# Expert weights of a routed decoder layer: all requested at the start, measured and split in earlier steps

## The reference, cut to what matters

```
x = layernorm(x + attention(x))             # 16 heads of 8, softmax, bias bo on the output
x = layernorm(x + retention(x, ctx, ctx))   # rotated queries and keys, decay mask, 16 heads of 8
x = layernorm(x + ffn(x))
ffn: 8 experts; each token takes its top 2 by x @ gate, softmax of the two logits as weights
     expert e: (silu(x @ w1[e]) * (x @ w3[e])) @ w2[e],  w1, w3: 128 x 512,  w2: 512 x 128
```

## Time and profile before

| | |
|---|---|
| median of the runs | 1030.12 us |
| profiled execution | 1043.64 us, span 1041.8 us from first to last instruction |
| busy over the span | PE 841.7, DVE 800.1, ACT 619.4, POOL 650.2 us |
| moved by DMA | 72.09 MB, mean 69 GB/s |
| mean granted clock of TensorE | 0.921 |

### The profile page before, as it was taken

One profiled execution on the slowest core, in us unless ns is written; L12 is line 12 of the kernel. 1 busy time (PEld: TensorE's weight loads), 2 busy tenths in 40 slices (PEclk: granted clock), 3 DMA queues, 4 the chain that ended last, 5 costly groups with the idle time before them and its releaser, 6 DMA issues.

```text
span 1041.8 us, 35968 instructions
## 1 busy us (share of the span) xinstructions
PE 841.7 (81%) x12164; PEld 632.6 (61%) x12165; DVE 800.1 (77%) x2219; ACT 619.4 (59%) x1416; POOL 650.2 (62%) x738
## 2 busy tenths in 40 slices
PE   1574879999999999988979760899999999999600
PEld 1342556666666666665655430788888888888500
DVE  3876889998889888978956644587878888778565
ACT  1132547667677676666666851566666666666445
POOL 0363957689889998989896456144444444444443
PEclk9796989999999999999998975899999999999955
DMA  7232312132222321212212002222212212212177
GB/s 240 59 75 66 69 30 49 32 73 54 58 64 52 70 63 48 68 33 63 48 48 62 23 27 82 53 63 58 57 57 58 58 56 61 58 53 61 34 253 228
DMA packets 145256, 72.09 MB, mean 69 GB/s; under 512 B 75024, under 2 KB 134544, under 8 KB 145136
## 3 DMA queue, kind: packets, MB, share of 16 engines
q1 hardware_dynamic: 124800, 40.56, 16.7%
q0 software_dynamic: 8640, 17.84, 5.1%
q10 hardware_dynamic: 11696, 12.08, 3.7%
HBM read 42.11 MB, written 28.34 MB: 68 GB/s over the span
## 4 chain that ended last, share of the span: by engine, by line
PE 33%; POOL 25%; issue 15%; DMA 3%; ACT 1%; SPq 1%; DVE 1%; POOLq 0%; another core or an unknown queue 0%; ACTq 0%; DVEq 0%
POOL prod_ev L1550 14%; PE QKV L770 9%; PE ST L770 9%; POOL routed_rows L1567 7%; PE XT L798 6%; PE SC L798 5%; POOL rs L1530 2%; DMA prod_ev<-token_halves 1%; PE YY L788 1%; DMA routed_rows<-xe,pos 1%; PE TR L788 1%; POOL frs L1612 1%; PE ST L640 1%; PE YY L588 1%; SPq L488 0%
## 5 line engine op out<-in xcount | busy, mean ns | idle before, releaser
L1550 POOL TENSOR_TENSOR prod_ev<-e_sb,q_v 128x512 f32<-128x512 f32 x256 | 296.1, 1189 | 85.1 <-PE YY L588 47.9
L1599 POOL DMA_INDIRECT token_halves<-w_new,tok_i x142 | 137.9, 971 | 39.7 <-issue 34.1
L1567 POOL DMA_INDIRECT routed_rows<-xe,pos x128 | 130.7, 1021 | 30.4 <-issue 30.0
L1150 DVE TENSOR_TENSOR prod_qk<-q_v,QKV 128x2048 f32<-128x2048 f32 x64 | 145.5, 2275 | 0.0
L1036 ACT ACTIVATE prod_qk<-QKV,silu_scale 128x512 f32<-128x512 f32 x142 | 95.1, 687 | 60.4 <-PE QKV L770 58.9
L1452 DVE TENSOR_TENSOR prod_ev<-prod_qk,prod_ev 128x1024 f16<-128x1024 f32 x71 | 87.0, 1225 | 54.7 <-ACT prod_ev L1027 35.2
L770 PE MATMUL QKV<-k_t,w_hl 128*128 128x256 f16 x852 | 117.4, 274 | 0.1
L770 PE MATMUL ST<-k_t,w_hl 128*128 128x256 f16 x852 | 117.0, 274 | 0.1
L411 POOL TENSOR_TENSOR marks<-half_c 128x1 f32<-128x1 f32 x103 | 19.7, 192 | 151.2 <-DVE w_new L1468 150.9
L1478 DVE SCALAR_TENSOR_TENSOR prod_qk<-ST,hid_scale,prod_qk 128x512 f32<-128x512 f32 x142 | 102.1, 744 | 10.0 <-ACT prod_qk L1036 6.5
L923 ACT ACTIVATE q<-XT,tab 128x256 f32<-128x256 f32 x256 | 96.6, 496 | 0.0
(11 more groups left out here) (169 smaller groups left out, 1776.7 us busy)
## 6 DMA issues: line engine op xcount, KB each, us to landing
w_new<-routed_rows SPq DMA_DIRECT2D x71, 130.0 KB
prod_ev<-token_halves SPq DMA_DIRECT2D x16, 512.0 KB, 5.0
x_sb<-x SPq DMA_DIRECT2D x32, 128.0 KB, 2.6
x_res<-x SPq DMA_DIRECT2D x128, 32.0 KB
head_rows<-o_n SPq DMA_DIRECT2D x32, 128.0 KB
o_t<-head_rows SPq DMA_DIRECT2D x64, 64.0 KB
ctx_sb<-ctx SPq DMA_DIRECT2D x32, 128.0 KB
out<-prod_qk ACTq DMA_DIRECT2D x16, 256.0 KB, 4.2
```

The source lines that it names most:

```text
L1150: eng.tensor_tensor(prod_qk[:, u, :, :].rearrange("p d (i j) -> p d i j", j=NH), q.unsqueeze(3).to_broadcast([P, HD, NH, NH]), k.unsqueeze ...
L1550: ins = eng.tensor_tensor(prod_ev[:, u, q, :, :, 0:HD], e_sb[:, it.slot(2), u, 64 * q:64 * q + 64].rearrange("p (i j) -> p j i", j=4).unsq ...
L1567: eng.indirect_dma_start(out=xs, out_offset=bass.IndirectOffsetOnAxis(ap=pos[:, r, 2 * u + k:2 * u + k + 1], axis=0), in_=xe[:, r, u, k, : ...
L1599: eng.indirect_dma_start(out=halves, out_offset=bass.IndirectOffsetOnAxis(ap=tok_i[:, s, u:u + 1], axis=0), in_=yw[:, s, u, :], in_offset= ...
```

## The change

All three matrices are requested by ScalarE before its first wait, in the order w1, w2, w3: six requests, 6 MB. w1 keeps `w_new`; w3 keeps `q8`; w2 goes to the memory of `w3_hl`, which is as large (two halves of 4096 float16 a partition) and is not needed for itself until the high half of w3 is written. The blank write stays at the end of ScalarE's step 0. The matrices are handled in the order w1, w2, w3, and the steps become (0, 3, 5), (3, 5, 7), (3, 5, 7), (4, 6, 8). The high half of w3 waits for the low half of w2 (`lo_ready` 2), and the first write of q8 in retention waits for `lo_ready` 3 where it waited for 2. SyncE no longer waits for `pool_consts` 2 ahead of the x tiles. TensorE starts on `consts_ready` 1 (the constants that VectorE copies at lines 1064 and 1065) and waits for `consts_ready` 2 (the bias rows) in `residual` of item 0. No instruction of arithmetic is added or removed.

```diff
--- before.py
+++ after.py
@@ -412,6 +412,8 @@
 
         def fresh(n):
 
+            if n == 2:
+                return w3_hl[:, :, :].rearrange("p k w -> p (k w)").bitcast(F32)
             return q8[:, :, :, :, :, :].rearrange("p s b u r t -> p (s b u r t)") if n == 1 else w_new[:, :]
 
         def norm_slot(c, d):
@@ -432,7 +434,8 @@
 
 
 
-        MEASURE, SPREAD_AT, HIGH, LOW, FETCH_LAST = (1, 3, 6), (3, 5, 8), (3, 5, 8), (4, 6, 9), 5
+        MEASURE, SPREAD_AT, HIGH, LOW = (0, 3, 5), (3, 5, 7), (3, 5, 7), (4, 6, 8)
+        WEIGHTS = (0, 2, 1)
         SPREAD = ST[:, 0:P]
 
         def pairs(ap):
@@ -450,8 +453,6 @@
             eng.dma_start(wo_sb[:, :], wo).then_inc(small_in, 16)
             eng.dma_start(bo_sb[:, :], bo).then_inc(small_in, 16)
             eng.dma_start(gate_sb[:, :], gate).then_inc(small_in, 16)
-
-            eng.wait_ge(pool_consts, 2)
 
             def step(at):
                 if it := at(0):
@@ -526,7 +527,7 @@
         def _(eng):
             eng.wait_ge(tab_in, 16)
             eng.wait_ge(small_in, 16 * 4)
-            eng.wait_ge(consts_ready, 2)
+            eng.wait_ge(consts_ready, 1)
 
             def tokens_across(it):
 
@@ -591,6 +592,8 @@
 
             def residual(it):
 
+                if it.i is None and it.off == 0:
+                    eng.wait_ge(consts_ready, 2)
                 wait_ring(it, y_in, per=96)
                 wait_last(it, n_duo, (x2t_ready, 5), (res1_ready, 1))
                 eng.matmul(Y, ones_bf[:, :], bo_bf[:, :], start=True, stop=False, skip_group_check=True)
@@ -701,12 +704,12 @@
 
             def spread_max(at):
 
-                for n in range(3):
-                    if at_step(at, SPREAD_AT[n]):
-
-                        eng.wait_ge(mats_ready, n + 1)
-                        if n > 0:
-                            eng.wait_ge(top_ready, n)
+                for k in range(3):
+                    if at_step(at, SPREAD_AT[k]):
+
+                        eng.wait_ge(mats_ready, k + 1)
+                        if k > 0:
+                            eng.wait_ge(top_ready, k)
                         eng.matmul(SPREAD, w_mats[:, :], ident, start=True, stop=True).then_inc(max_spread, 1)
 
             def step(at):
@@ -813,7 +816,6 @@
         @block.scalar
         def _(eng):
             w2_parts = w2.rearrange("e (n p) h -> n p e h", p=P)
-
             def load_weights(n):
 
                 if n < 2:
@@ -821,8 +823,11 @@
                                   (w1, w3)[n].rearrange("e h i -> h e i")).then_inc(w_in[n], 16)
                 else:
                     for k in range(n_chunk):
-                        eng.dma_start(w_new[:, :].rearrange("p (e n h) -> p e n h", e=n_exp, n=n_chunk)[:, :, k, :],
+                        eng.dma_start(fresh(n).rearrange("p (e n h) -> p e n h", e=n_exp, n=n_chunk)[:, :, k, :],
                                       w2_parts[k]).then_inc(w_in[n], 16)
+
+            for n in WEIGHTS:
+                load_weights(n)
 
             eng.wait_ge(tab_in, 16)
             eng.wait_ge(small_in, 16 * 4)
@@ -830,20 +835,16 @@
             def weights(at):
 
                 if at_step(at, 0):
-                    load_weights(0)
-                    load_weights(1)
 
                     eng.wait_ge(blank_ready, 1)
                     eng.dma_start(xs[n_exp * region:n_exp * (region + TILE), :].rearrange("(n p) c -> p n c", p=P),
                                   spare_rows).then_inc(blank_out, 16)
-                if at_step(at, FETCH_LAST):
-
-                    eng.wait_ge(lo_ready, 1)
-                    load_weights(2)
-                for n in range(3):
-                    if at_step(at, HIGH[n]):
-
-                        eng.wait_ge(scale_ready, n + 1)
+                for k, n in enumerate(WEIGHTS):
+                    if at_step(at, HIGH[k]):
+
+                        eng.wait_ge(scale_ready, k + 1)
+                        if k == 2:
+                            eng.wait_ge(lo_ready, 2)
                         eng.activation((w1_hl, w3_hl, w2_hl)[n][:, 0, :], fresh(n), ACT.Copy,
                                        scale=w_scale[:, n:n + 1]).then_inc(hi_ready, 1)
 
@@ -918,7 +919,7 @@
                 wait(it, st_done[1], 2)
                 wait_last(it, n_duo, (qt_done, 0), (xt_done, -9), (kt_done, 0))
                 if it.i is None and it.off < 2:
-                    eng.wait_ge(lo_ready, 2)
+                    eng.wait_ge(lo_ready, 3)
                 for r in range(HD):
                     ins = eng.activation(q8[:, it.slot(2), :, :, r, :].rearrange("p b u t -> p (b u) t"),
                                          QT.rearrange("p (n t) -> p n t", t=S), ACT.Copy,
@@ -1106,18 +1107,18 @@
 
             def weights(at):
 
-                for n in range(3):
-                    if at_step(at, MEASURE[n]):
+                for k, n in enumerate(WEIGHTS):
+                    if at_step(at, MEASURE[k]):
 
                         eng.wait_ge(w_in[n], 16 * (1 if n < 2 else n_chunk))
                         link(eng.tensor_reduce(w_high[:, n:n + 1], fresh(n), AX.X, ALU.max, apply_absolute_value=True))
-                        if n > 0:
-                            eng.wait_ge(max_spread, n)
+                        if k > 0:
+                            eng.wait_ge(max_spread, k)
                         eng.tensor_copy(w_mats[:, :], w_high[:, n:n + 1].to_broadcast([P, P])).then_inc(mats_ready, 1)
-                for n in range(3):
-                    if at_step(at, LOW[n]):
-
-                        eng.wait_ge(hi_ready, n + 1)
+                for k, n in enumerate(WEIGHTS):
+                    if at_step(at, LOW[k]):
+
+                        eng.wait_ge(hi_ready, k + 1)
                         hl = (w1_hl, w3_hl, w2_hl)[n]
                         eng.scalar_tensor_tensor(out=hl[:, 1, :], in0=fresh(n), scalar=w_scale[:, n:n + 1], in1=hl[:, 0, :],
                                                  op0=ALU.mult, op1=ALU.subtract).then_inc(lo_ready, 1)
@@ -1130,13 +1131,13 @@
 
             def weight_scales(at):
 
-                for n in range(3):
-                    if at_step(at, SPREAD_AT[n]):
+                for k, n in enumerate(WEIGHTS):
+                    if at_step(at, SPREAD_AT[k]):
 
                         one = slice(n, n + 1)
-                        eng.wait_ge(max_spread, n + 1)
+                        eng.wait_ge(max_spread, k + 1)
                         eng.tensor_reduce(w_top[:, one], SPREAD, AX.X, ALU.max).then_inc(top_ready, 1)
-                        eng.wait_ge(top_ready, n + 1)
+                        eng.wait_ge(top_ready, k + 1)
                         link(eng.tensor_scalar(w_max[:, one], w_top[:, one], TINY, None, ALU.max))
                         link(eng.reciprocal(w_inv[:, one], w_max[:, one]))
                         eng.tensor_scalar(w_scale[:, one], w_inv[:, one], W_SCALE, None, ALU.mult).then_inc(scale_ready, 1)
```

## The result

| | before | after |
|---|---|---|
| median of 20 runs | 1036.8 us (1025.23 to 1046.1) | 1028.42 us (1021.45 to 1031.8) |
| profiled execution | 1043.64 us | 1025.35 us, span 1023.5 |
| ratio to before | 1 | 0.9918, 95% interval 0.9899 to 0.9936 |

The kernel after is faster by 0.8%, 8.4 us between the medians; a change of 12.3 us was forecast. With 20 runs the kernel before has a median 6.7 us above that of the three runs shown ahead of the prediction, so the forecast of 1018 us, made against 1030.1, lies 10 us under what was measured. That 1028.42 lies within the stated range of 1008 to 1031 is no support for the working: the range was laid round that lower median.

A forecast was written before the change was run, and what follows sets the result against it. Holes in filling the pipeline, followed along VectorE's weight work, were taken as the bound. Saving 8.5 us in steps 5 to 9 and 3.8 at the start, 12.3 off 1030.1, gave 1018 us, range 1008 to 1031.

The forecast's parts named there:

- The start: Filling's beginning: ScalarE's last weight request taken at 15.8 us, products of item 0 at 22.0 instead of 25.77, 3.8 us saved.
- the rival of cheap requests: Start: requests interleave plainly, ScalarE free at 7 us, products at 18.0, 16 to 18 us saved, 1013 us; chance 0.17.
- The rate of 0.33 MB/us: Start: assumed transfer rate, read as 0.66 MB in 2 us, used to time when requests are taken and data land.
- 3,650 outstanding rows: ScalarE's requests: about 3,650 rows taken as what the queue holds before the next request blocks.
- my 4.54: Start: 4.54 MB to land before the last weight request is taken, which at 0.33 gave 15.8 us.
- a request of SyncE does not slip past a blocked one: Start: SyncE's small inputs come later behind ScalarE's blocked request; 13 us taken for them.
- The bias rows' edit: TensorE's first transpose no longer waits for the bias rows; priced at nothing, since ScalarE is blocked past that.
- Steps 3 and 4 keep their work ... and their length: Filling, steps 3 and 4: w2's maximum replaces w3's, so no change in length.
- Step 7 gains a scale of 0.9 us at most: Step 7: the scale lies beneath a wait of 1.28 us, TensorE comes in warmer; 9.8 us for 10.17.
- Steps 5 and 6: Step 5 takes over a maximum, 13.15 us for 8.55; step 6 loses w2's wait and the maximum, 13.4 for 24.94.
- Steps 8 and 9: Step 8 gets the low half of w3, 19.4 us for 10.31; step 9 gives it up, 11.2 for 21.48.
- The sum: Steps 5 to 9 at 66.95 us for 75.45 save 8.5; with the start's 3.8, 12.3 us in all.

The follow-up runs named there:

- late_req: The kernel after, but all six weight requests issued at the end of ScalarE's step 0, ahead of the blank write; ratio to before 0.9906.
- paced: The kernel after with only w1 requested at the start, w2 and w3 at the end of ScalarE's step 1; ratio to before 0.9903.
- no_bias: The kernel after with both start waits of before put back (TensorE for the bias rows, SyncE for pool_consts); ratio to before 0.9913.
- bias_only: The kernel before with only the change's two start waits altered, weights requested where they were; ratio to before 0.9967.
- warm: The kernel after with 17 filler matmuls, results never read, where TensorE waits for m_own in steps 4, 5, 6, 7, 9; ratio to before 0.9888.
- warm_again: The same kernel as warm, after with 17 filler matmuls, run once more in another group; ratio to before 0.9851.
- after_again: The kernel after, unchanged, run and traced again; ratio to before 0.9925.
- before_again: The kernel before, unchanged, run and traced again as a control; ratio to before 1.0024.
- group 2: Second of three groups of follow-up runs, holding after_again, before_again and no_bias among others; its own runs of before have a median of 1035.99 us.

## Why the prediction was wrong, step by step

**The start: the blocking was forecast, its working was wrong in two places, and its gain was lost again.** Forecast: ScalarE's last weight request taken at 15.8, products at 22.0. Measured: 17.51 and 23.55; the rival of cheap requests falls. The rate of 0.33 MB/us was right, the 3,650 outstanding rows were not. They can be counted in the DMA view, where a packet is a row, but for a few small ones; q10 is ScalarE's queue and q1 SyncE's, with packets and MB. Before, from 72.01 to 77.32 us, while w2 was requested:

```profile
q10 hardware_dynamic: 1979, 1.00, 73.6%
```

So 1,979 of the 4,096 rows of w2 had landed by 77.32, and 2,117 were left, where I took 5.8 us x 0.33 = 1.9 MB, 3,700 rows. The other row, of the blank write, stands: 3,495 by count. After, from 0 to 17.51 us, when the last weight request was taken:

```profile
q10 hardware_dynamic: 3644, 3.41, 62.4%
q1 hardware_dynamic: 1808, 1.72, 34.2%
```

So 2,500 of the 6,144 rows were outstanding, and as many in late_req (3,637 landed at 20.11 us). One fixed number of rows thus does not describe where a request blocks: 3,495 with the blank write's short rows among them, 2,500 with w2's. With 3.41 + 1.72 = 5.13 MB for my 4.54 the sum gives 17.5 us, as measured. The second fault is in "a request of SyncE does not slip past a blocked one" as the cause of the late small inputs: paced has them as late with no request blocked.

The bias rows' edit was worth nothing beside the requests (no_bias), as forecast. What I did not draw from this: the two edits work against each other. The first frees the first transpose from 11 to 6.8 us (bias_only), the second moves it back to 12.8. Requesting at the start earned nothing over requesting behind the first transpose (late_req).

Of the 3.8 us that the start was to bring, the products had 2.2, the start of step 3 had 1.8 and the start of step 4 0.8: "Steps 3 and 4 keep their work ... and their length" failed in step 3, 14.29 for 13.26. Its length too goes largely with the clock: 13.26 or 13.27 us at 0.87 (before, late_req, warm), 14.29 at 0.76 (after), 14.85 and 15.05 at 0.66 and 0.65 (warm_again, no_bias); but after_again has 13.92 at 0.88.

**The step that failed is "Step 7 gains a scale of 0.9 us at most ...; TensorE comes in warmer. I take 9.8".** It measured 14.02 and 12.09, the largest part of the error in both traces. I had taken the hole of 16 us before step 7 for the cause of a lower clock, and a shorter hole for a cure. The hole is this wait in before:

```profile
92.86 0.79 PE L570 MATMUL YY<-m_own,tab 128*128 128x128 f32 x2 [16.26 <-DVE m_own L1160]
```

But the change leaves in its place gaps of 3.5 to 4.9 us at the start of steps 5, 6, 7 and 9, and in after TensorE went through steps 5, 6 and 7 at 0.76, 0.88 and 0.52 of its clock (after_again: 0.88, 0.86, 0.62), and at 0.50 in the stretch where its sums and scores end the step. warm shows it by intervention: gaps filled, clock 1.00, step 7 at 9.13, under my 9.8. The kernel before is not free of this: with its long hole, bias_only has its step 7 at 0.62 and 12.09 us. The Trainium skill ("TensorE: Matmul & The Clock Gate", section "What's actually happening") says that idling brings the lower level and that how long one kernel stays cold at its start varies from run to run. The traces agree in the filling, with steps 5 of 8.55 and 10.99 and steps 7 of 14.02 and 12.09 in the same kernels.

**Steps 5 and 6** measured 14.08 and 15.11 for 13.15 and 13.4. With the clock up they are 13.07 and 14.15, so 1 us of each is the clock too. Of the 0.75 left in step 6, 0.68 is the low half of w2, 5.16 for 4.48, beside GpSimd's multiplications. Steps 8 and 9 (18.85, 10.86) were within 0.6 of 19.4 and 11.2.

**The sum.** Steps 5 to 9 took 72.92 for 66.95, so 2.5 us were saved in the pair of traces instead of 8.5; with the start's 0.8 the lead at step 10 was 3.3 us, for 12.3. With the clock up they take 65.4 us (warm) and 65.3 (warm_again), which is below the 66.95: the term was right for a TensorE at full clock, and the lower clock takes 6.3 to 7.6 us (71.66 in after_again, 72.92 in after).

Part of the error lay in the yardstick: the trace of before that I priced from had step 5 at full clock (8.55; 10.99 and 10.92 in before_again and bias_only), and step 10 at 134.08 where before_again has 137.36. In group 2 the lead at step 10 is 137.36 - 129.17 = 8.2 us, 6.9 from steps 5 to 9 and 1.3 from the start, and the time is 0.75% less, 7.8 us. In the first pair the lead is 3.3 and the medians are 8.4 apart. One trace of each kernel is thus too few to add the gain up to the microsecond; that the change gains 8 us comes from the 20 runs.

**What stays open.** The 18 us between the first two traces hold 14 of the stretch from step 10 to stage B (517 and 503 us). That stretch differs by up to 23 us between groups and by up to 7 within one, so much of the 14 may be chance; whether the kernel after also gains a few microseconds there is not settled. Nor do the runs show what makes one execution of a kernel fall to the lower clock in a step and another not.

## What to carry to other kernels

A hole that is cut up may cost more than its remainder: look at the clock in the window where TensorE's work ends the step, and price the following steps at either level, since here the same step ran at both. Price an early transfer by what its issue does to the engine that issues it and by what its bytes do to other queues' requests, and ask what else needed that moment. Count the packets that have landed instead of working them out from a rate that was read elsewhere. One trace of a filling pipeline is a poor yardstick for microseconds, since its steps may be at either clock.

## What the runs showed that I had not expected

- A VectorE instruction and GpSimd's slow each other: eight multiplications take 13.23 us beside the low half of w2 (5.16 us instead of 4.48), 9.03 and 9.04 us in the steps around. The Trainium skill ("SBUF — State Buffer", section "Summary: rules for kernel authors") says that when a VectorE instruction with two inputs in that memory meets a GpSimd one that reads it, the later to issue blocks until the other is done. The 4.2 us more on GpSimd, nearly the 4.48 of the low half, agree.
- Even one request of 2 MB at 0.71 us (paced) moved the landing of the first x tile from 6.8 us (bias_only) to 12.8, as much as six did.
